# The last of eight attention periods written in another order on five engines of one Trainium2 core

## What is computed

```python
x = x + linear_attention(layernorm(x))
x = x + cross_attention(layernorm(x), ctx, ctx)        # "values" and "sums" below
h = layernorm(x)
logits = h @ Wg.T
top_v, top_i = top_k(logits, 2); gates = softmax(top_v)
pos = cumsum(onehot(top_i)) - 1                        # the place of a row in its expert's batch
exp_batches[expert, pos] = h                           # dropped where pos >= 1280
y = (gelu(a) * b) @ W2[e],  a, b = split(exp_batches[e] @ W1[e])
x = x + sum over the two experts of gate * y
```

## Time and profile before

| | |
|---|---|
| median of 3 runs | 1505.38 us (1504.08 to 1509.91) |
| the profiled execution, its own time | 1506.71 us |
| its span | 1504.8 us |
| PE busy | 1434.2 us, 95% of the span |
| DVE, ACT, POOL busy | 655.2, 614.5, 378.5 us |
| chain of work that ended last | PE 86%, DMA 4%, DVE 3%, issue 2%, ACT 2%, POOL 2% |
| DMA | 135.58 MB, mean 90 GB/s |

### The profile page before, as it was taken

The page is one execution under the profiler, slowest core; times in us unless marked ns, Lnnn a source line. Parts: engine busy times, 40 slices in busy tenths (PEclk is TensorE's granted clock), DMA queues, the critical chain, the costliest instruction groups (busy, mean ns, idle before and its releaser), DMA issues.

```text
span 1504.8 us, 22275 instructions
## 1 busy us (share of the span) xinstructions
PE 1434.2 (95%) x7496; PEld 1215.0 (81%) x7497; DVE 655.2 (44%) x1448; ACT 614.5 (41%) x1032; POOL 378.5 (25%) x374
## 2 busy tenths in 40 slices
PE   5999999999976889999999999999999999999997
PEld 4768887787865778888988888899889888898886
DVE  6635666668886635211532531255422331253111
ACT  4534554257766535212532532255423432253222
POOL 3302232127665431111212112022212112021111
PEclk9999999999996889999999999999999999999999
DMA  9310221219566654221532532055414332053112
GB/s 203 43 78 29 84 85 56 84 54 222 120 141 183 169 139 102 91 35 15 160 91 45 140 95 42 7 134 181 91 76 98 91 91 42 7 133 70 16 39 28
DMA packets 82163, 135.58 MB, mean 90 GB/s; under 512 B 32546, under 2 KB 32674, under 8 KB 81092
## 3 DMA queue, kind: packets, MB, share of 16 engines
q1 hardware_dynamic: 64484, 97.67, 23.8%
q0 software_dynamic: 17632, 37.30, 13.1%
HBM read 94.42 MB, written 40.53 MB: 90 GB/s over the span
## 4 chain that ended last, share of the span: by engine, by line
PE 86%; DMA 4%; DVE 3%; issue 2%; ACT 2%; POOL 2%; another core or an unknown queue 0%; SPq 0%; ACTq 0%; POOLq 0%; DVEq 0%
PE pg L1045 16%; PE pg L1047 16%; PE pg L1046 16%; PE pj L1045 9%; PE pj L1047 9%; PE pj L1046 9%; PE pt L1443 2%; PE pj L1280 2%; PE pg L1308 1%; DMA slot_table<-pack,dest 1%; PE pg L1246 1%; POOL slot_table L634 1%; DMA out_rows<-ost,etab 1%; PE pt L1063 1%; PE pt L1267 1%
## 5 line engine op out<-in xcount | busy, mean ns | idle before, releaser
L1045 PE MATMUL pg<-xe_hi,w_hi 128*128 128x512 f32 (+2 forms) x1152 | 402.7, 350 | 9.3 <-issue 7.3
L1046 PE MATMUL pg<-xe_lo,w_hi 128*128 128x512 f32 (+2 forms) x1152 | 402.1, 349 | 0.0
L1047 PE MATMUL pg<-xe_hi,w_lo 128*128 128x512 f32 (+2 forms) x1152 | 402.1, 349 | 0.0
L1985 DVE TENSOR_TENSOR hp<-gl,pg 128x512 f32<-128x512 f32 x136 | 93.5, 687 | 577.9 <-ACT gl L1016 565.9
L732 POOL DMA_INDIRECT out_rows<-ost,etab x62 | 98.0, 1580 | 736.4 <-ACT ost L1000 363.3
L1045 PEld LDWEIGHTS pg<-xe_hi,w_hi 128*128 128x128 f32 x1152 | 219.7, 191 | 36.2 <-issue 11.1
L1046 PEld LDWEIGHTS pg<-xe_lo,w_hi 128*128 128x128 f32 x1152 | 219.8, 191 | 25.1
L1047 PEld LDWEIGHTS pg<-xe_hi,w_lo 128*128 128x128 f32 x1152 | 219.6, 191 | 24.9
L1016 ACT ACTIVATE gl<-pg 128x512 f32<-128x512 f32 x136 | 81.3, 598 | 372.3 <-PE pg L1047 363.6
L1045 PE MATMUL pj<-w_hi,hg_hi 128*128 128x512 f32 x448 | 177.1, 395 | 0.0
L1047 PE MATMUL pj<-w_hi,hg_lo 128*128 128x512 f32 x448 | 174.5, 390 | 0.0
(11 more groups left out here) (266 smaller groups left out, 2048.5 us busy)
## 6 DMA issues: line engine op xcount, KB each, us to landing
stage<-w SPq DMA_DIRECT2D x96, 512.0 KB
xr<-x SPq DMA_DIRECT2D x8, 1024.0 KB, 10.9
out_rows<-xr SPq DMA_DIRECT2D x8, 1024.0 KB, 8.8
x_rows<-xn SPq DMA_DIRECT2D x8, 1024.0 KB
x_in<-x SPq DMA_DIRECT2D x7, 1024.0 KB, 5.3
x_rows<-zrow POOLq DMA_DIRECT2D x1, 2304.0 KB
late_xT<-xT_hi SPq DMA_DIRECT2D x2, 1024.0 KB, 3.9
late_xT<-xT_lo SPq DMA_DIRECT2D x2, 1024.0 KB, 5.9
```

The source lines that it names most:

```text
L1045: nc.tensor.matmul(o, lh, rh, start=start, stop=False)
L1046: nc.tensor.matmul(o, lh, rl, start=False, stop=False)
L1047: return nc.tensor.matmul(o, ll, rh, start=False, stop=stop)
L1985: v.tensor_tensor(hp[j % 2][:], gl[j % 2][:], pg[:, 2 + j % 2, :], ALU.mult).then_inc(s_hp, 1)
```

## The change

The change moves work between neighbouring places in these lists; the matmuls, vector operations and transfers stay the same in number and size.

- PE, last period: all four `values` come ahead of `turn_soon` and `positions` (before: `turn_soon`, two values, `positions`, two values). Down: tile 0 waits piece by piece for W2 (before: for all twelve pieces at its start), and the loop's registers are set after tile 0 (before: after the last transposes).
- DVE, last period: `cross_out` comes ahead of the early rows' `xe_lo`, the places and their packing (before: behind them).
- ACT, last period: pieces 4 and 5 are split behind the first two GELUs (before: ahead of `squares_3`).
- SP: the early table is read ahead of period 6's `out_rows` store (before: behind it). In the last period the store of `out_rows` goes ahead of piece 6. `etab_next` is read ahead of pieces 10 and 11, and no longer waits for the two stores.
- POOL: the two waits that SP gave up stand now ahead of the first gathers (`s_x3`) and ahead of `add_soon` (`s_out`). `gather_soon` is called at the end of period 6 (before: at the start of period 7).

```diff
@@ -464,17 +464,16 @@
 
                     sp.wait_ge(s_o, GROUPS * TI)
                     first_pieces(range(STG))
-                if g == GROUPS - 1:
-                    first_pieces(range(STG + 2, STG + 3))
+                if g == SOON:
+
+                    sp.wait_ge(s_scat, 16 + 16 * TI * TOPK * SOON)
+                    sp.dma_start(etab_soon[:], table_t[:, 0:SOON_TILES]).then_inc(s_etab, 16)
                 sp.wait_ge(s_x2t, (g + 1) * TI)
                 sp.dma_start(out_g[g], xr[g % 4][:]).then_inc(s_out, 16)
                 if g == SOON:
-
-                    sp.wait_ge(s_scat, 16 + 16 * TI * TOPK * SOON)
-                    sp.dma_start(etab_soon[:], table_t[:, 0:SOON_TILES]).then_inc(s_etab, 16)
                     first_pieces(range(STG, STG + 2))
                 if g == GROUPS - 1:
-                    first_pieces(range(STG + 3, STG + 6))
+                    first_pieces(range(STG + 2, STG + 6))
                 for q in range(2):
                     if g == q:
 
@@ -488,11 +487,9 @@
                 if g + 4 < GROUPS:
                     sp.wait_ge(s_out, 16 * (g + 1))
                     sp.dma_start(xr[g % 4][:], x_g[g + 4]).then_inc(s_xr[g % 4], 16)
-            first_pieces(range(STG + 6, WP))
-            sp.wait_ge(s_out, 16 * GROUPS)
-            sp.wait_ge(s_x3, 16 * GROUPS)
             sp.wait_ge(s_scat, 16 + 16 * TI * TOPK * GROUPS)
             sp.dma_start(etab_next[:], table_t[:, SOON_TILES:SOON_TILES + ET]).then_inc(s_etab, 16)
+            first_pieces(range(STG + 6, WP))
 
             for i in range(CHUNKS[0]):
                 sp.wait_ge(s_xg0[i], 16)
@@ -667,8 +664,6 @@
             sigma(0)
             late_q(late(-1, 1))
             for g in range(GROUPS):
-                if g == SOON + 1:
-                    gather_soon()
                 if g >= 1:
                     scatter(g - 1, range(0, TI * TOPK - 2))
                 late_q(late(g - 1, 2))
@@ -683,6 +678,8 @@
                 norm3(g)
                 if g + 1 < GROUPS:
                     sigma(g + 1)
+                if g == SOON:
+                    gather_soon()
                 late_q(late(g, 1))
             scatter(GROUPS - 1, range(TI * TOPK // 2, TI * TOPK))
 
@@ -695,12 +692,14 @@
 
             pool.wait_ge(s_meta, 1)
             pool.wait_ge(s_etab, 32)
+            pool.wait_ge(s_x3, 16 * GROUPS)
             pool.wait_ge(s_xet, SOON_TILES)
             for i in range(CHUNKS[0]):
                 p.indirect_dma_start(
                     out=xg[:, i, :], out_offset=None, in_=x3d,
                     in_offset=bass.IndirectOffsetOnAxis(ap=etab_next[:, i, 0:1], axis=0)).then_inc(s_xg0[i], 16)
             scatter_last_gates()
+            pool.wait_ge(s_out, 16 * GROUPS)
             add_soon()
             for i in range(CHUNKS[0]):
                 pool.wait_ge(s_xg0[i], 16)
@@ -939,7 +938,7 @@
                     turned_rows(xT2, range(2, TI), 1)
                 if g == GROUPS - 1:
                     rows_hi(0, range(SOON_TILES))
-                    for s in range(2, STG + 2):
+                    for s in range(2, STG):
                         split(0, s)
                 squares_3(g)
                 if g == GROUPS - 2:
@@ -960,7 +959,10 @@
                 if j >= 1:
                     act.wait_ge(s_hp, j)
                     a.activation(soon_hi[:, j - 1, :], hp[(j - 1) % 2][:, 0:SOON_SLOTS], ACT.Copy).then_inc(s_hghi, 1)
+                if j == 0:
+                    split(0, STG)
                 if j == 1:
+                    split(0, STG + 1)
                     split(0, STG + 2)
                 if j == 2:
                     normalise3(GROUPS - 1)
@@ -1346,17 +1348,16 @@
                 if more_groups:
                     attend(g + 1, range(2, TI))
                 sums(g, at_e)
-                if not more_groups:
-                    turn_soon()
                 if more_groups:
                     at_x1 = turn_x1(g + 1, range(2))
                 late_q(g, 0)
                 values(g, range(2))
                 if more_groups:
                     at_x1.update(turn_x1(g + 1, range(2, TI)))
+                values(g, range(2, TI))
                 if not more_groups:
+                    turn_soon()
                     positions(g)
-                values(g, range(2, TI))
                 if more_groups:
                     positions(g)
                     scores(g + 1, at_x1)
@@ -1389,28 +1390,29 @@
                         ins = three(pg[:, 2 * half + j % 2, 0:SOON_SLOTS], w1_hi[:, j, k, m], w1_lo[:, j, k, m],
                                     xe_hi[:, k, 0:SOON_SLOTS], xe_lo[:, k, 0:SOON_SLOTS], k == 0, k == KC - 1)
                 ins.then_inc(s_h, 1)
-            pe.wait_ge(s_w_lo, WP)
+
+
+
+            at_e, at_c, at_left, at_first, at_done, at_next = (
+                pe.alloc_register(f"pe_{n}") for n in ("expert", "chunk", "left", "first", "done", "count"))
             pe.wait_ge(s_sinv, GROUPS)
             pe.wait_ge(s_posev, GROUPS)
             for i in range(SOON_TILES):
                 m = slice(i * P, (i + 1) * P)
                 for j in range(FJ):
                     if i == 0:
+                        pe.wait_ge(s_w_lo, W1P + j // 2 + 1)
                         pe.wait_ge(s_hglo, j + 2)
                     ins = three(pj[i][:], soon_hi[:, j, m], soon_lo[:, j, m], w2_hi[:, j, :], w2_lo[:, j, :],
                                 j == 0, j == FJ - 1)
                 ins.then_inc(s_y, 1)
+                if i == 0:
+                    pe.wait_ge(s_meta, 1)
+                    for r, value in ((at_e, 0), (at_c, 0), (at_first, SOON_TILES), (at_done, FJ)):
+                        pe.reg_mov(r, value)
+                    pe.reg_load(at_left, meta[0:1, 0, 0:1])
                 turn_first_rows(range(2 * i, 2 * i + 2))
 
-            pe.wait_ge(s_meta, 1)
-
-
-
-            at_e, at_c, at_left, at_first, at_done, at_next = (
-                pe.alloc_register(f"pe_{n}") for n in ("expert", "chunk", "left", "first", "done", "count"))
-            for r, value in ((at_e, 0), (at_c, 0), (at_first, SOON_TILES), (at_done, FJ)):
-                pe.reg_mov(r, value)
-            pe.reg_load(at_left, meta[0:1, 0, 0:1])
             with pe.Fori(0, EX * len(CHUNKS)):
                 with pe.If(pe.snap(at_e, min_val=0, max_val=EX) < EX):
                     e = pe.snap(at_e, min_val=0, max_val=EX - 1)
@@ -1910,11 +1912,11 @@
                     gates(g)
                     pack_tokens(g)
                 else:
+                    cross_out(g)
                     rows_lo_of(0, range(SOON_TILES))
                     positions_out(g)
                     slots(g)
                     pack_last_tokens()
-                    cross_out(g)
                     for s in range(2, STG):
                         split(0, s)
 
```

## The result

| | before | after |
|---|---|---|
| median (lowest to highest) of 8 runs each, us | 1505.64 (1502.48 to 1509.91) | 1496.56 (1492.97 to 1504.46) |
| ratio, 95% interval | | 0.9946 [0.993, 0.9963] |
| the same two kernels measured again, 27 and 12 runs | 1507.15 | 1503.09; ratio 0.9969 [0.9957, 0.9981] |
| profiled execution (span), us | 1506.71 (1504.8) | 1492.97 (1490.9) |

A forecast was written before the change was run, and what follows sets the result against it. PE bounds the loop, so its entry at 544.08 us decides: 7.5 us from values first plus 4.4 from down give 12.0 us, the rest neutral, hence 1493.4 us; range 1489.0 to 1499.4.

The forecast's parts named there:

- The likeliest case: The forecast itself: loop entered 12.0 us earlier, 1493.4 us, own range 1491.9 to 1494.9, chance 0.54.
- Values first: PE, last period: four values before the early rows' transposes start up at 486.9 instead of 494.44, 7.5 us gained.
- Pieces during up: Up: remainders arrive in time, PE does not stall, and up keeps its 24.8 us.
- early table: SP: read ahead of the store, gathers start some 2 us sooner; only cover, costed at nothing.
- Down: Down's tile 0: the 2.98 us wait goes and the clock stays full, another 4.4 us gained.
- the next step: Regular rows' table: scatters land at 505, POOL gathers 10.0 us earlier, PE does not wait; pieces 10 and 11 keep their lead.
- Rival A: Regular rows' table late: scatters take 8.98 us, PE waits 3.4 us for rows; gain 8, 1497.4 us, chance 0.17.
- Rival D: Slower: SP holds pieces 10 and 11 until scatters land after about 520; 1509 us with 23 us landing, chance 0.05.
- The entry: From the last regular transposes to the loop's first matmul the 7.30 us stay; moving the register load gives nothing.
- rival B: Loop entry: the 4.00 us of issue were the register load's latency and go; gain 16.0, 1489.4 us, chance 0.10.
- Behind the entry: Loop's first chunk: ACT's split of expert 1's pieces up to 2.0 us late, cost at most 0.3 us; caps the gain.
- The loop: Loop over experts: PE is busy in all 910 us at full clock, and its length does not depend on its start.

The follow-up runs named there:

- after again: After, unchanged, measured and profiled once more: 1503.09 us, ratio 0.9969 to before.
- the split: After, with the third and fourth regular rows' transposes moved behind the third step of down's second tile: 1502.54 us, ratio 0.9956 to before.
- the next expert's early pieces: After with pieces 10 and 11 ahead of the regular table, plus expert 1's first four pieces asked for before the gates' wait: 1501.31 us, ratio 0.9958.
- the pieces ahead of the table: After, with pieces 10 and 11 asked for ahead of SP's scatter wait and the regular table's read: 1498.45 us, then 1499.23 us.

## Why the prediction was right, and where it was wrong

The sign, the place and the range held in the first measurement: 1496.56 us lies in 1489.0 to 1499.4. The likeliest case's own range, 1491.9 to 1494.9, missed. That the range held is in part luck: the second measurement, 1503.09 us with a gain of 4, a third of the forecast, lies outside it.

*Values first* was right: 10.46 us from the sums to up were forecast and 10.14 measured, the same within 0.14 in all twelve executions with this order. The values ran at the lower level, as assumed, and the early rows were there.

*Pieces during up* was right: no stall of PE in up in either execution of after. Up took 25.8 and 25.0 us against 24.8, longer by the lower clock. The cover of the *early table* held too, but the store's place on SP, costed at nothing, is what keeps the DMA engines busy early. Values first without the rest of the change gained 2.4 us of 7.9 at the loop, and putting piece 6 back ahead of the store cost 3.5 us at the loop against after again. I looked at when the store's end is waited for and not at what stands behind it.

***Down* is the step that failed.** It was worth 4.4 us in the first profiled execution, as forecast, and −0.5 in the second (from up's end to tile 0's end 5.6 and 10.5 us, against 10.0 before). It said that the remainders move with up, 7.5 us earlier, to 514.7 for a need at 515.9, and the next step said that pieces 10 and 11 "keep their lead". By its own rows they don't: their issue moves by about 3 us (505.5 for 508.43) and their need by 7.5. ACT began to split piece 10 8.2 us after SP asked for it in before, and 4.3 in the first execution of after:

```profile
508.85 2.73 SPq L460 DMA_DIRECT2D stage<-w  x2
517.00 1.05 ACT L913 ACTIVATE w_hi<-stage 128x1024 fp32r<-128x1024 f32 x1
```

```profile
507.66 1.05 ACT L912 ACTIVATE w_hi<-stage 128x1024 fp32r<-128x1024 f32 x1
```

In after again the same piece took 4.6 us from SP's issue to the end of ACT's wait, so the first execution's 4.3 had nothing to spare. The step rested on a landing at 505, 28.6 us after the sums. The first profiled execution landed at 29.1 and lost nothing; after again at 33.9, near the bound of 509.4 (33.0) that I had taken in, and there tile 0 ended 45.7 instead of 41.5 us after the sums. The nine other runs built on after asked for the table at 32.1 to 36.2. So the value I took, "nearer the empty price", was the rare one among the profiled executions: in the ten others the scatters land in 6.3 to 9.6 us.

*Rival A* had the right cause, late scatters, and put the wait at the regular rows. Its 1497.4 is near the first median by luck, as far as is known: the one profile of that measurement shows early scatters. *Rival D* had the right queue, SP in front of pieces 10 and 11, and let it decide from a landing after 520. With D's own 8 us from landing to the last remainder, the need at 515.9 is missed from 507.9 on, 31.5 us after the sums, and A's 509.4 lies beyond that. The runs agree: no wait at 29.1 and 3.4 us at 33.7, so the wait begins, if each microsecond of landing costs one, at 30 to 31 (an estimate from the five executions with this order that waited, 33.7 to 36.2 for 3.1 to 4.9 us). D asked when the change turns slower and not from when it loses. The two belonged together, with the larger chance.

*The entry* was nearly right in its size, 8.1 and 7.9 us for 7.3, and wrong in its reading. I split 7.30 us into 3.3 for `xe_lo` and 4.00 of issue. In the eleven executions without the split or the next expert's early pieces the gap is 6.9 to 8.8 us from PE's last work, and in nine of them the last `xe_lo` ended 1.9 to 5.1 us ahead of the loop; with the split it ended before PE's last matmul, and 6.3 and 7.8 us remained. Only in two, both with the pieces ahead of the table, did the profile name `xe_lo`, which ended 0.1 and 0.7 us ahead of the loop. Moving the register load changes the gap by 0.7 us at most, so rival B falls. In every execution a packet of instructions arrives within 2 us of the end of PE's last work and another behind it. The Trainium skill (Runtime: NRT & Kernel Launch, Instruction fetch mechanics) says that a taken branch out of the fetched window waits for its page by DMA. The runs fit that and don't show it: with the gap of 11.3 us the packets were 7 us apart, but in the other eleven they were 3 to 6.5 apart without order (5.5 with a gap of 7.3, 3.5 with 8.7). The 200 ns for a register that the Trainium skill gives in the same section are within what the move of the load could have shown. What fills the gap stays open.

*Behind the entry*: expert 1's pieces were 1.6 and 1.7 us late for ACT in the two executions of after and cost PE nothing, as said. That they cap the gain was not shown: asked for 19 us earlier, they gave nothing.

*The loop* kept its length: 960.7 us from its first matmul to the span's end before, 960.0 after; from 560 to 1466 PE is busy in all 906 us at the full clock.

## What to carry to other kernels

When an engine's start moves forward, list every queue that feeds it, and check that each issue moves with it: an in-order queue that waits for a transfer with a variable landing holds everything behind it, so what is needed first goes ahead of that wait. For a duration with two prices in the trace, take the one measured under the load that the change makes, and work out from which value on it costs anything, not only from where the sign turns. One profiled execution can be the lucky one; a second profile of the same kernel showed the wait that the first had not.

## What was not expected of the hardware

- At the loop's entry PE stands 6.9 to 8.8 us in the eleven executions without the split or the next expert's early pieces, and 15 matmuls queued ahead cover at most a microsecond or two of it; no run here shows what the time is spent on.
- In the one execution with 2 MB of weights asked for 5 us ahead of the last transposes the gap was 11.3 us and the two packets of instructions came 7 us apart (3 in both executions of after). The DMA engines moved 116 GB/s in this gap and 40 in that of after again. That their load lengthens the entry is likely from this and not shown by one execution.
- The eight token scatters land 4.9 to 9.6 us after the start of the last one in kernels built on after, and 4.9 and 6.8 in two executions of after itself; no run here shows why.
- Up's first matmuls ran at the lower level for 3.6 us in before and for 6 in the first execution of after. In the eleven other executions with the values first it was 3.3 to 4.4 us in eight, and in three up was at the full level almost from its start; in before and after the level rose under matmuls that followed each other without a gap.
